# First-layer attention scores from two f16 parts, 32 rows a head and four heads at once on TensorE

## What is computed

```
x = x + attn0(ln(x)) + ffn0(ln(x))     # attn0: 32 query heads, 8 key/value heads, head size 8, rope,
                                       #        causal softmax over 1024 keys, float32
                                       # ffn0: fp8 operands, gelu(gate) * up, then down
x = x + attn1(ln(x)) + ffn1(ln(x))     # attn1: 16 heads over 512-row sequences, softmax over the heads
                                       #        of one position; ffn1: ternary weights, silu, rms norm
scores0 = einsum('bhqd,bhkd->bhqk', rope(q), rope(k)) / sqrt(8)
```

## Time and profile before

| | us |
|---|---|
| median of 3 runs | 645.83 |
| the three runs | 644.84, 645.83, 756.25 |
| the profiled execution's own time | 643.59 |
| its span, first to last instruction | 641.8 |
| mean granted TensorE clock, share of full | 0.988 |

### The profile page before, as it was taken

How to read it: one execution, slowest core, us unless ns; L and a number is a source line. 1 busy time by engine, 2 the same in 40 slices (tenths; PEclk the granted TensorE clock), 3 DMA queues, 4 the chain that set the end, 5 groups by cost and what they waited for, 6 DMA issues and landing times. The chain is left out here.

```text
span 641.8 us, 13919 instructions
## 1 busy us (share of the span) xinstructions
PE 592.7 (92%) x5195; PEld 304.4 (47%) x5245; DVE 437.3 (68%) x901; ACT 498.0 (78%) x941; POOL 275.3 (43%) x415
## 2 busy tenths in 40 slices
PE   3579989999999999999999999999999999999882
PEld 1334344345354455554554445554454444446661
DVE  6699988887557666667888677663554467357664
ACT  2289989897988988998698885778988987885340
POOL 5687826556332026335866653503141442132100
PEclk9799999999999999999999999999999999999997
DMA  8701010031210414104000022432213013044440
GB/s 290 274 2 34 34 34 2 1 50 35 34 34 1 67 20 77 29 3 73 12 0 28 1 24 44 75 51 56 21 34 42 1 26 50 27 66 83 69 64 30
DMA packets 150923, 30.48 MB, mean 47 GB/s; under 512 B 133952, under 2 KB 149568, under 8 KB 150848
## 3 DMA queue, kind: packets, MB, share of 16 engines
q1 hardware_dynamic: 150272, 29.19, 22.8%
q10 hardware_dynamic: 576, 0.33, 0.2%
HBM read 19.02 MB, written 10.49 MB: 46 GB/s over the span
## 5 line engine op out<-in xcount | busy, mean ns | idle before, releaser
L888 ACT ACTIVATE Pt<-psS 128x512 f32<-128x512 f32 x576 | 298.5, 621 | 37.8 <-PE psS L637 29.7
L652 PE MATMUL psV<-Pt,vaug 128*32 128x512 f32 x1152 | 146.1, 601 | 1.8 <-POOL Pt L1508 0.8
L1508 POOL TENSOR_SCALAR_AFFINE_SELECT Pt<-Pt 128x512 f32<-128x512 f32 x128 | 87.5, 721 | 54.7 <-ACT Pt L888 54.5
L637 PE MATMUL psS<-qT,kT 49*128 49x512 bf16 x576 | 96.7, 382 | 1.8 <-ACT Pt L888 0.5
L637 PEld LDWEIGHTS psS<-qT,kT 49*128 49x128 bf16 x576 | 22.9, 94 | 84.1 <-ACT Pt L888 44.0
L652 PEld LDWEIGHTS psV<-Pt,vaug 128*32 128x32 f32 x1152 | 26.5, 108 | 54.6 <-issue 41.7
L1563 POOL TENSOR_TENSOR ss<-ss,mhalf 128x1 f32<-128x1 f32 x16 | 9.3, 580 | 86.2 <-DVE ss L1344 86.2
L936 ACT ACTIVATE stage<-psS 128x512 f32<-128x512 f32 x64 | 33.0, 603 | 13.5 <-PE psS L755 13.5
L1477 POOL TENSOR_TENSOR rt<-qkv,cs 128x320 f32<-128x320 f32 x16 | 14.9, 930 | 37.4 <-DVE qkv L1100 36.8
L1218 DVE SCALAR_TENSOR_TENSOR ga<-gw,gb 128x512 bf16<-128x512 f32 x32 | 26.4, 824 | 4.6 <-ACT gw L913 4.6
L1350 DVE SCALAR_TENSOR_TENSOR qtmp<-qtmp,ss 128x1024 f16<-128x1024 f32 x16 | 23.0, 1436 | 5.3 <-ACT qtmp L956 5.3
(11 more groups left out here) (354 smaller groups left out, 1325.2 us busy)
## 6 DMA issues: line engine op xcount, KB each, us to landing
qkvscr<-rqkv SPq DMA_DIRECT2D x16, 384.0 KB, 2.6
G<-qkvscr SPq DMA_DIRECT2D x48, 128.0 KB, 3.7
stage<-in_wg SPq DMA_DIRECT2D x4, 512.0 KB, 8.2
oscr<-o SPq DMA_DIRECT2D x16, 128.0 KB, 3.0
at<-oscr SPq DMA_DIRECT2D x16, 128.0 KB, 2.1
out<-yout SPq DMA_DIRECT2D x16, 128.0 KB, 2.3
x<-in_x SPq DMA_DIRECT2D x1, 1536.0 KB, 12.0
r<-in_wgu SPq DMA_DIRECT2D x2, 512.0 KB, 8.1
```

What stands on the lines that cost most here:

```text
L637: e.matmul(psS[j][:], kT[64 * f:64 * f + 49, j, 128 * at:128 * at + 128], qd[64 * f:64 * f + 49, 4 * j:4 * j + 4, :].rearrange("p s n -> p ...
L652: ins = e.matmul(psV[32 * j:32 * j + 32, :], vaug[:, at, j, 32 * f:32 * f + 32], Pt[(4 * Q + j) % NP][:], start=(kb == 0 and h == 0), stop ...
L888: e.activation(Pt[u % NP][:], psS[j][:], ACT.Exp, scale=SC0).then_inc(S["exp"], 1)
L1508: e.affine_select(out=p, in_=p, pattern=[[0, 4], [1, 128]], compare_op=ALU.is_ge, fill=0.0, base=0, channel_multiplier=-1).then_inc(S["mas ...
```

## The change

- q and k, rotated, are scaled up by 64 and split into two f16 parts, high and low, in place of three bf16 parts. A head has 32 rows in place of 64: q as (high, high, low, low) and k as (high, low, high, low). The 49th row, a constant shift, is gone. It is now the bias of the exp, a tile `low` of one column. The exp's scale takes out the 64 * 64.
- The four matmuls of a quad have 32 rows each and start at rows 0, 32, 64 and 96.
- qh writes 512 elements, q0 128, and the two new steps kl (DVE) and ql (POOL) write the low parts. qr, qm, q1 and q2 are gone.
- A tile needs 10 blocks transposed in two steps (2 for k, 8 for q), and kTc copies 256 columns and one qTc 1024.
- QX has two buffers and qT four (halves of the buffers that the second pass uses in f32). POOL's memsets of QX are gone.
- Columns of wqkv are permuted on the host. The rope then runs over plain heads: same element count and instruction count.
- New on DVE in each tile: wide, the largest magnitude of q and k before rope (128x320 reduced). The flag also tests it, which adds two small instructions at the end.
- The loads of bqkv, cs0 and sn0 have semaphores of their own: qkv waits for wqkv alone.
- The second pass multiplies its scores in f32 with 9 rows a head.
- All five lists in ORDER are laid out anew.

The core of the diff:

```diff
             def qk(Q):
                 n, kb, h = QUADS[Q]
...
                 for j in range(4):
-                    f = (j + h) % 2
                     scores_free("qk", Q, j)
-                    e.matmul(psS[j][:], kT[64 * f:64 * f + 49, j, 128 * at:128 * at + 128],
-                             qd[64 * f:64 * f + 49, 4 * j:4 * j + 4, :].rearrange("p s n -> p (s n)"), start=True,
+                    e.matmul(psS[j][:], kd[32 * j:32 * j + k, h, 128 * at:128 * at + 128],
+                             qd[32 * j:32 * j + k, 4 * h:4 * h + 4, :].rearrange("p s n -> p (s n)"), start=True,
                              stop=True).then_inc(S["qk"], 1)
...
+                for at, u in enumerate(range(8) if part else range(8, 10)):
+                    ins = e.transpose(bank[:, at, :], src[:, 4 * u:4 * u + 4, :].rearrange("p r c -> p (r c)"), identh[:])
...
             def qh(n):
-                e.activation(X3[:, 0:32, 0:24].rearrange("p h (c d) -> p h c d", d=8), heads(rt[n % len(rt)], 0, 0, 32, 3),
-                             ACT.Copy).then_inc(S["qh"], 1)
+                    e.activation(cells(QX[n % len(QX)])[:, 0:32, 0:2, :], heads(src, 2), ACT.Copy).then_inc(S["qh"], 1)
-            def qm(n):
...
-                e.activation(Pt[u % NP][:], psS[j][:], ACT.Exp, scale=SC0).then_inc(S["exp"], 1)
+                        e.activation(Pt[u % NP][:], psS[j][:], ACT.Exp, bias=low[:], scale=SC0 / UP / UP).then_inc(S["exp"], 1)
...
+            def wide(n):
+                    e.tensor_reduce(widest[:, n:n + 1], qkv_b[n % len(qkv_b)][:, 0:320], AX.X, ALU.max,
+                                    apply_absolute_value=True).then_inc(S["wide"], 1)
...
+            def kl(n):
+                e.tensor_tensor(X4[:, 32:40, 1:4:2, :], heads(rt[n % len(rt)][:, 0, 256:320], 2), X4[:, 32:40, 0:4:2, :],
+                                ALU.subtract).then_inc(S["kl"], 1)
...
+            def ql(n):
+                e.tensor_tensor(X4[:, 0:32, 2:4, :], heads(rt[n % len(rt)][:, 0, 0:256], 2), X4[:, 0:32, 0:2, :],
+                                ALU.subtract).then_inc(S["ql"], 1)
```

More of the change, by code:

```diff
@@ L29 @@
 SHIFT = -45.25
+UP = 64.0
+WIDEST = 600.0
 MAGIC = 12582912.0
@@ L211, in one_round @@
     steps = []
-    for word in ROUND[engine].split():
+    for word in (ROUND if n < NT else ROUND2)[engine].split():
         if word == "QUADS":
@@ L261, in score_banks @@
     return dict(zip(fills[1:], fills))
-SEMS = """d_x0 d_x1 d_x2 d_id d_w0 d_c d_w1 d_wg0 d_wg1 d_gu0 d_gu1 d_vw0 d_vw1 d_vr d_ow d_or d_out0 d_out1
-xnT qkv qxT mT obT attT wo0 up down xn1T qkv1 gT S1m gTagain S1 PV1 o1T at1T wo1 gu hxT dn1 ts td tr qk pv rmm flagT
-qh qm exp g sq fh th qk1c gTk ex1 tg ssq hxa tc tde sin
-idc vz tab cst w8 w8m w8s tsc tm tcs tw ln0 xn xnTc qkvc va q0 q1 kTc qTc rmax rcomb mxn mTc ob att attTc xa ge1 ge3 ge3b a8c yff
+SEMS = """d_x0 d_x1 d_x2 d_id d_b d_cs d_w0 d_c d_w1 d_wg0 d_wg1 d_gu0 d_gu1 d_vw0 d_vw1 d_vr d_ow d_or d_out0 d_out1
+xnT qkv qxT fxT mT obT attT wo0 up down xn1T qkv1 gT S1m gTagain S1 PV1 o1T at1T wo1 gu hxT dn1 ts td tr qk pv rmm flagT
+qh exp g sq fh th qk1c gTk ex1 tg ssq hxa tc tde sin
+idc vz tab cst w8 w8m w8s tsc tm tcs tw ln0 xn xnTc qkvc va wide q0 kl kTc qTc fTc rmax rcomb mxn mTc ob att attTc xa ge1 ge3 ge3b a8c yff
 ln1 xn1 xn1Tc v1c ro1 ro2 gTq m1 gTm o1r o1 sg hh ssm hx hTc at1Tc yo yout ysum flag
-zero gz rs0 rope qr q2 mask ge4 xf rs1 xl ro1p rsg w8a""".split()
+zero gz zf rs0 rope ql mask ge4 xf rs1 xl ro1p rsg w8a""".split()
 class Waits:
@@ L524, in sp @@
             all_landed(1)
-            w.wait_ge("flag", 12)
+            w.wait_ge("flag", 14)
             again = e.value_load(flag[0:1, 0:1], min_val=0, max_val=1)
@@ new lines, in qxT, with transpose_heads, fxT @@
+                ins.then_inc(S["qxT"], 1)
+            def transpose_heads(bank, units, sem):
+                for at, u in enumerate(units):
+                    ins = e.transpose(bank[:, 128 * at:128 * at + 128],
+                                      QXf[:, 4 * u:4 * u + 4, :].rearrange("p r c -> p (r c)"), identf[:])
+                ins.then_inc(S[sem], 1)
+            def fxT(m):
+                n, part = divmod(m, 3)
+                w.wait_ge("qh", n + 1)
+                w.wait_ge("q0", n + 1)
+                transpose_heads(shared("fxT", m), (range(8, 10), range(0, 4), range(4, 8))[part], "fxT")
@@ L602, in rmm @@
             def rmm(n):
-                qd = qT[n % 2]
-                w.wait_ge("kTc", n + 1)
-                w.wait_ge("qTc", 2 * n + 2)
+                qd = qTf[n % 2]
+                w.wait_ge("fTc", 3 * (n - NT) + 3)
                 scores_free("rmm", n, 3)
                 R = chunk_count(n)
-                for s in range(16):
-                    for f in range(2):
-                        for at, k in chunks(n):
-                            w.wait_ge("rmax", R - 3)
-                            e.matmul(psS[R % 4][:, 0:128 * k], qd[64 * f:64 * f + 48, s, :],
-                                     kT[64 * f:64 * f + 48, s // 4, 128 * at:128 * at + 128 * k], start=True,
-                                     stop=True).then_inc(S["rmm"], 1)
-                            R += 1
+                for s in range(32):
+                    u, r = divmod(s, 4)
+                    for at, k in chunks(n):
+                        w.wait_ge("rmax", R - 3)
+                        e.matmul(psS[R % 4][:, 0:128 * k], qd[32 * r:32 * r + 8, u, :],
+                                 kTf[32 * r:32 * r + 8, u // 4, 128 * at:128 * at + 128 * k], start=True,
+                                 stop=True).then_inc(S["rmm"], 1)
+                        R += 1
@@ L887, in exp @@
                     w.wait_ge("pv", (u - NP) // 4 + 1)
-                    e.activation(Pt[u % NP][:], psS[j][:], ACT.Exp, scale=SC0).then_inc(S["exp"], 1)
+                    if n < NT:
+                        e.activation(Pt[u % NP][:], psS[j][:], ACT.Exp, bias=low[:], scale=SC0 / UP / UP).then_inc(S["exp"], 1)
+                    else:
+                        e.activation(Pt[u % NP][:], psS[j][:], ACT.Exp, scale=SC0).then_inc(S["exp"], 1)
             def g(m):
@@ new lines, in qTc, with fTc @@
+            def qTc(n):
+                bank = psM[filled["qxT", 2 * n + 1] % len(psM)][:].bitcast(F16).rearrange("p (s n) -> p s n", n=128)
+                w.wait_ge("qxT", 2 * n + 2)
+                if n >= len(qT):
+                    w.wait_ge("qk", 4 * QUAD_END[n - len(qT)])
+                e.tensor_copy(qT[n % len(qT)], bank).then_inc(S["qTc"], 1)
+            def fTc(m):
+                n, part = divmod(m, 3)
+                at = n % NT % RING
+                bank = psM[filled["fxT", m] % len(psM)]
+                w.wait_ge("fxT", m - 3 * NT + 1)
+                w.wait_ge("pv", max(keys_free(n), QUAD_END[NT - 1]) if part == 0 else 0)
+                w.wait_ge("qk", 4 * QUAD_END[n - 2])
+                dst = kTf[:, :, 128 * at:128 * at + 128] if part == 0 else qTf[n % 2][:, 4 * part - 4:4 * part, :]
+                e.tensor_copy(dst, bank[:, 0:256 if part == 0 else 512].rearrange("p (u n) -> p u n", n=128)).then_inc(
+                    S["fTc"], 1)
@@ new lines, in rmax @@
+                for s in range(32):
+                    for c, (at, k) in enumerate(runs):
+                        bank = psS[R % 4]
+                        w.wait_ge("rmm", R + 1)
+                        w.wait_ge("rmax", R)
+                        if c + 1 < len(runs):
+                            e.reduce_max(mxp[:, c, s:s + 1], bank[:, 0:128 * k], AX.X).then_inc(S["rmax"], 1)
+                            if c > 0:
+                                w.wait_ge("rmax", R + 1)
+                                w.wait_ge("rcomb", C)
+                                e.tensor_tensor(mxp[:, 0, s:s + 1], mxp[:, 0, s:s + 1], mxp[:, c, s:s + 1],
+                                                ALU.max).then_inc(S["rcomb"], 1)
+                                C += 1
+                        else:
+                            w.wait_ge("rcomb", C)
+                            e.tensor_tensor_reduce(
+                                out=mjunk[:, s % 2, 0:128], in0=bank[:, 0:128], in1=mneg[:], scale=1.0,
+                                scalar=mxp[:, 0, s:s + 1] if c > 0 else NEG, op0=ALU.add, op1=ALU.max,
+                                accum_out=mx[:, s:s + 1]).then_inc(S["rmax"], 1)
+                        R += 1
@@ L1391, in out_of_range @@
                 w.wait_ge("ysum", NT)
+                w.wait_ge("wide", NT)
+                e.tensor_reduce(hl[:, 8:9], widest[:], AX.X, ALU.max).then_inc(S["flag"], 1)
                 e.tensor_reduce(hl[:, 0:1], ra, AX.X, ALU.max).then_inc(S["flag"], 1)
@@ L1625 @@
     rows = [((16 * f + 4 * j + h) * 8 + d) for h in range(4) for j in range(4) for f in range(2) for d in range(8)]
+    order = [((16 * f + 4 * r + h) * 8 + d) for f in range(2) for h in range(4) for r in range(4) for d in range(8)]
     arrays = {
```

(4 more changed lines are left out.)

258 lines of the change are left out of this document (116 added, 142 removed), and 271 rows, old and new, of tables (ORDER, ROUND).

## The result

| | before | after |
|---|---|---|
| median, us (9 runs each) | 645.83 | 650.09 |
| span of the profiled execution, us | 641.8 | 649.2 |
| mean granted TensorE clock | 0.988 | 0.978 |

The ratio of after to before is 1.0074, with a 95% interval from 1.0052 to 1.0097. The kernel is 0.7% slower. I had said 610 us, in a range from 598 to 630. One run of before, 756.25 us, lies apart and is in no comparison.

What follows compares the result with a forecast made beforehand. PE was taken to bound the middle (98.6% busy, 120 to 600 us). From 643.6 us: -4 start, -4 from 40 to 120, -26 middle, 0 tail, +0.25 flag; sum -34, 609.8, stated 610 us, range 598 to 630.

Steps and rivals of the forecast that it cites:

- the exps' bias, counted at 0: ACT, exps: the bias becoming a tile adds nothing; another 0.01 us an exp would put 5.8 us on ACT.
- the allowance of a fifth for late banks: PE, 120 to 600 us: a fifth of the 32.8 us saving is lost where banks are unread, leaving 26.
- ACT takes over: Rival, 120 to 600 us: ACT keeps its 82% share, the middle gains only 12 us, time 624 us; chance 0.15.
- four at a time: PE, score matmuls: a quad's four run at once, saving 0.22 us a quad, 31.7 us over 144 quads.
- The rival of four signals: Rival, PE scores: four completion signals cost time, the gain is 0.15 us a quad, time 618 us; chance 0.10.
- two at a time: Rival, PE scores: matmuls still go in pairs, 0.44 us a quad with no gain, time 632 us; chance 0.07.
- one after another: Rival, PE scores: 32-row 16-bit matmuls run singly, 0.88 us a quad, 63 us lost, time 690 us; chance 0.02.
- the work behind the last quad: Behind 600 us: 13 more PE steps fall where PE had 15 us idle; work moved, counted at 0.
- the start: 0 to 40 us: scores start near 26.2 us and exps near 26.7, counted as 4 us less.
- the split's single steps: ACT, POOL, DVE, each tile: qh 0.65 us, ql 1.2, kTc about 0.25; ACT saves 13.9 us in all, DVE 5.
- My own tests: Wrong if quads take 0.5 us, middle PE idle grows over 15, exps start over 0.51 apart, or tail outgrows its steps.
- The last line of the sum: Whole kernel: terms sum to -34 from 643.6, giving 609.8 us; median 2.2 us above the profiled execution, stated as 610.

## Why the prediction was wrong, step by step

**The step that failed: the exps' bias, counted at 0.** I wrote that the trace has a memset of a constant 0.0, "so I take it that an activation reads a bias already: 0". The row said no such thing: a constant that is written is not a constant that an exp reads, and the names in the exps' own row list psS alone. The term measures 0.10 us times 576, 57 us on ACT at most and 52 by its groups, and some 24 us of the time. My upper price of 0.01 us an exp was a tenth of it. The experiments show this term by itself, in both families, and it is the difference between 0.7% slower and 2.9% faster. What followed from it was wrong with it: 484 us for ACT, and with ACT's pace the allowance of a fifth for late banks.

The trace of before had the price, in two activations one after another of the same size, one of which has a bias tile (hpi); count, then min, median and max ns:

```profile
L852 ACT ACTIVATE sin<-ang x1: 256/256/256, 92.4 to 92.4; 128x64 f32<-128x64 f32 x1
...
L853 ACT ACTIVATE cos<-ang,hpi x1: 333/333/333, 92.6 to 92.6; 128x64 f32<-128x64 f32 x1
```

That is 0.077 us for a tile at 64 elements. At 1024 elements an activation with a scale tile took 1.175 us (qtmp, L956), and one without took 1.057 (L859): 0.12. At 512 elements the runs have 0.10. So it hardly depends on the size. 0.08 to 0.12 times 576 is 44 to 68 us on ACT, and with that my rival "ACT takes over" should have been the forecast. The Trainium skill, "ScalarE: Activation LUTs", section "What ACT_TABLE_LOAD costs", states it outright: "each `[128,1]` pointer operand adds ≈ 93 ns" over numbers in the instruction. An estimate by that figure is 54 us on ACT for one tile. The runs agree: an exp lasts 0.096 to 0.107 us longer for one tile and 0.193 for two, and exps that follow one another start 0.477, 0.570 and 0.663 us apart with none, one and two.

**Right: four at a time.** I took four at once and a change of kind of 0.10 us; a free quad took 0.40 us, its four starts lay within 0.01 us, and the next kind followed after 0.32. The rival of four signals had it at 0.39. Neither that nor two at a time nor one after another happened in a free quad.

**Right without the tile, wrong with it: a fifth lost to late banks.** I wrote that a quad's four go together "only if all four banks were read" and let a fifth be lost. Without the tile 5.8 of the quads' 31.7 us were lost (31.7 - 25.9), 18%. With it 30 of them were (0.654 to 0.642).

**Wrong: the work behind the last quad, "counted at 0".** I put the moved steps at 0 in the tail, on the ground that PE had 15 us idle there. The 16 us of work did not go into that idle time: PE was idle for 16.9 us behind the last exp before, and for 20.7 after without a bias. Windows of fixed borders hide this. The attention ended 38 us earlier without a bias (544 in place of 582), and 15 earlier with it (567), while the span ends at 624 and 649. The moved work has to be done there, in serial chains of layer two in which PE fills 74% (59.3 of 80), not the 96% of the middle (498.1 of 517). At the middle's share the 16 us of work would need 17 us, not 20: the other 3 are lost. The comparison of lists says the same (23 us taken out of the middle, 20 put into the tail, for 15 us of PE's work). That the chains are the reason was not tested; in the two kernels that shortened the DMA's part of them nothing was won.

So of the 16 us between 610 and 626, some 3 are the tail's. None are the quads' or the transposes': their groups fell by 24 us and by 11 (25.3 to 14.1), and the sum had 34 for the two. PE's idle time between the first and the last exp is 18.9 us where before had 14.7, and some 4.5 of the 14.7 stand for missing records, so 9 are gaps that I hadn't counted. The lists of before have as many (18.2), so they come with the faster data path and not with the new order. ACT's share of that stretch rose from 86% (471.9 of 549) to 88% (457.0 of 517); that PE waits more for a fuller ACT fits, but no run parts this from other reasons. The remaining 4 or so I can't assign. That the kernel without a bias comes near the 624 us of the rival "ACT takes over" settles nothing. From 120 to 600 us ACT has 394.2 us, the 82% that this rival gave it, but the last 56 us of that window lie behind the last exp; between the exps its share rose.

**Right: the start.** Scores were to start near 26.2 us and exps near 26.7. They started at 26.41 and 26.89. That gave 6 us against the old first exp at 33.15, of which I counted 4; by PE's work that moved, 3 of the 6 are real.

**Right: the split's single steps.** Rows of after for three of them, to lay beside the earlier trace rows (min, median and max ns):

```profile
L892 ACT ACTIVATE QXf<-rt x16: 629/680/768, 16.2 to 457.4; 128x512 f16<-128x512 f32 x16
```

```profile
L1535 POOL TENSOR_TENSOR QXf<-rt,QXf x16: 1149/1164/1707, 16.9 to 473.4; 128x512 f16<-128x512 f32 x16
```

```profile
L1161 DVE COPY kTf<-psB x6: 273/282/291, 26.1 to 487.0; 128x256 f16<-128x256 f16 x6
```

I had 0.65 us for the first, 1.2 for ql and 0.25 for kTc. ACT without the tile has 487.8 us (484 foreseen) and POOL lost 10 (0.6 a tile foreseen). DVE's sum was to fall by 5 us and rose by 1.4; other operations on it took longer, such as the product into gw, 830 ns each where it had 729 (L1251, before L1209). It has 65% of the stretch from 120 to 600 us before and 66% after.

**The rival "ACT takes over"**, laid beside after, had the place right and the reason wrong. I gave it 624 us, at ACT's old busy time less the split's part. Its condition, that ACT can't be filled further, holds in the stretch from 280 to 320 us of after:

```profile
280.00:320.00 40.00, 38.68 (x359) 20.04 (x358) 28.32 (x60) 39.75 (x73) 20.29 (x31) 1.00 0.25 31
```

**My own tests.** I said I'd be wrong if exps started more than 0.51 us apart. The mark was misread: 2.04/4 counts the last exp's own end, and exps that followed one another started 0.478 us apart. They now start 0.570 apart, four take 2.42 to 2.47 us, and the mark catches it by either figure. The quad's mark (0.5 us) catches it too, with a mean of 0.642, and so do the sums of PE and ACT. The part behind the last quad grew by 22.5 us (59.9 to 82.4) for 18 us of PE's work. The mark of 15 us for PE's idle time would not have caught it: from 120 to 600 us it grew by 12 (6.7 to 19.1).

**The last line of the sum.** 609.8 us stood for the profiled execution, and the median was said to lie 2.2 us above it. That makes 612, not 610.

## What to carry to other kernels

- An operand that turns from a number into a tile of one column is a change of price for every instruction that reads it. Look in the trace for two rows of the same shape with and without such an operand before you call it free. Here the same shift given as a number made the kernel 2.7% faster than before (627.32 us, 0.9734 [0.9696, 0.9772]), and it beats both kernels.
- Where the producer's results go into banks that a consumer frees one by one, a group made shorter only gains where all its banks are free. How many are free depends on the consumer's pace: here 0.09 us more an exp took all but 2 of 26 us. Count the groups that already wait before multiplying a saving by their number.
- Compare an engine's busy time in two profiles only after looking at the counts. Where weight loads and matmuls differ, records are missing, and their places look idle.
- When an order of work is laid out anew, compare stretches between events (first and last exp), not between fixed times, and subtract the work that changed sides.

## What the hardware did that I had not expected

- A tile of one column as bias costs an activation 0.10 us at 512 elements, and one as scale costs the same again (624, 720, 817 ns; from start to start 477, 570, 663). A bias given as a number costs nothing (624 ns with and without).
- Four matmuls of 32 rows at the row positions 0, 32, 64 and 96, with f16 operands and 512 columns, each with its own signal, ended together after 0.39 to 0.40 us; two of 49 rows had taken 0.39. Less the 0.10 us at the change of kind, the 0.32 us to the next kind leave 0.22 for 2048 columns, an estimate. S1's 32 matmuls put 4096 columns into PSUM in 0.90 us. So the pace is about twice that of S1.
